# Cross-attention block on one core: place of the bias rows' picks, and order of the products in the projections of contexts

## What is computed

```
def _cross_attention(q_in, kv_in, wq, bq, wk, bk, wv, bv, wo, bo, bias_k, bias_v):
    qh = (q_in @ wq + bq).reshape(b, q_len, H, K)
    kh = (kv_in @ wk + bk).reshape(b, t, H, K)
    vh = (kv_in @ wv + bv).reshape(b, t, H, K)
    kh = concatenate([kh, bias_k], axis=1)      # one bias row behind the 1500 keys
    vh = concatenate([vh, bias_v], axis=1)
    logits = einsum('bqhk,bthk->bhqt', qh, kh) / scale
    weights = softmax(logits, axis=-1)
    ctx = einsum('bhqt,bthk->bqhk', weights, vh).reshape(b, q_len, H * K)
    return ctx @ wo + bo

x = x + _cross_attention(layer_norm(x), context, ...1)
x = x + _cross_attention(layer_norm(x), context, ...2)
x = x + gelu(layer_norm(x) @ w_fc1 + b_fc1) @ w_fc2 + b_fc2
```

## Time and profile before

| | us |
|---|---|
| three runs without profile, median (lowest to highest) | 1191.36 (1190.72 to 1191.61) |
| the profiled execution | 1191.98 |
| its span (first to last instruction) | 1190.2 |
| PE busy in the span | 1178.3 (99%) |
| PE weight loads busy | 1098.7 (92%) |
| DVE, POOL, ACT busy | 893.2, 870.5, 770.4 |
| share of PE in the chain that ended last | 95% |
| of it line 808 (scores) | 39% |
| of it line 773 (projections) | 6% |

### The profile page before, as it was taken

How to read it: one execution, slowest core, us unless ns; L and a number is a source line. 1 busy time by engine, 2 the same in 40 slices (tenths; PEclk the granted TensorE clock), 3 DMA queues, 4 the chain that set the end, 5 groups by cost and what they waited for, 6 DMA issues and landing times.

```text
span 1190.2 us, 26498 instructions
## 1 busy us (share of the span) xinstructions
PE 1178.3 (99%) x7664; PEld 1098.7 (92%) x7664; DVE 893.2 (75%) x1654; ACT 770.4 (65%) x1514; POOL 870.5 (73%) x741
## 2 busy tenths in 40 slices
PE   8999999999999999999999999999999999999999
PEld 7788999999999999998998999999999999999898
DVE  6888768686867687777786877777777777777854
ACT  6756666666666666676685666666666666667766
POOL 4659778787878788677552878787969696967772
PEclk9999999999999999999999999999999999999999
DMA  5311222222222222233330122222222222222331
GB/s 166 114 56 53 64 73 62 73 61 73 60 74 59 75 59 75 48 72 94 96 98 19 40 63 74 61 75 58 75 58 74 60 74 60 72 50 72 71 102 44
DMA packets 148299, 83.62 MB, mean 70 GB/s; under 512 B 121181, under 2 KB 122605, under 8 KB 148249
## 3 DMA queue, kind: packets, MB, share of 16 engines
q1 hardware_dynamic: 147560, 82.23, 26.8%
q10 hardware_dynamic: 688, 0.80, 0.2%
HBM read 68.56 MB, written 0.53 MB: 58 GB/s over the span
## 4 chain that ended last, share of the span: by engine, by line
PE 95%; DVE 2%; ACT 1%; issue 1%; DMA 1%; DVEq 0%; SPq 0%; ACTq 0%
PE psum L808 39%; PE psum L815 14%; PE psum L821 14%; PE psum L816 13%; PE psum L773 6%; PE psum L861 5%; PE psum L787 3%; PE psum L721 1%; DVE g_prod L1354 1%; PE psum L737 0%; DVE oth L1597 0%; PE psum L842 0%; ACT oth L1202 0%; PE psum L760 0%; DVE t_max L1463 0%
## 5 line engine op out<-in xcount | busy, mean ns | idle before, releaser
L628 POOL TENSOR_TENSOR pt<-slots,pt 125x512 fp32r<-125x512 f32 (+3 forms) x384 | 454.2, 1191 | 155.4 <-ACT slots L1125 149.4
L808 PE MATMUL psum<-qs,ctx 128*125 128x384 f32 (+1 forms) x2304 | 527.5, 367 | 0.4 <-ACT slots L1144 0.4
L808 PEld LDWEIGHTS psum<-qs,ctx 128*125 128x125 f32 x2304 | 397.2, 186 | 40.4 <-ACT slots L1144 1.0
L815 PE MATMUL psum<-ctx,pt 125*128 125x258 f32 (+1 forms) x1344 | 378.5, 283 | 0.7 <-ACT on L1132 0.6
L816 PE MATMUL psum<-ctx,pt 125*128 125x256 f32 (+1 forms) x1344 | 376.9, 282 | 0.0
L821 PE MATMUL psum<-ctx,pt 125*128 125x258 f32 (+1 forms) x1344 | 369.4, 282 | 0.0
L1122 ACT ACTIVATE pt<-slots 125x512 fp32r<-125x512 f32 (+3 forms) x384 | 221.5, 577 | 220.6 <-DVE slots L1447 216.5
L1463 DVE TENSOR_TENSOR t_max<-psum,t_max 125x512 f32<-125x512 f32 (+1 forms) x282 | 175.4, 622 | 152.6 <-PE psum L808 150.6
L815 PEld LDWEIGHTS psum<-ctx,pt 125*128 125x128 f32 (+1 forms) x1344 | 253.5, 189 | 12.9 <-ACT on L1132 2.5
L816 PEld LDWEIGHTS psum<-ctx,pt 125*128 125x128 f32 (+1 forms) x1344 | 254.2, 189 | 6.5
L821 PEld LDWEIGHTS psum<-ctx,pt 125*128 125x128 f32 (+1 forms) x1344 | 250.5, 190 | 0.3 <-POOL pt L628 0.2
(11 more groups left out here) (115 smaller groups left out, 1032.9 us busy)
## 6 DMA issues: line engine op xcount, KB each, us to landing
tr_stage<-ctx_tr SPq DMA_DIRECT2D x60, 375.0 KB, 3.2
nat_stage<-ctx_nat SPq DMA_DIRECT2D x60, 375.0 KB
w_raw<-weights SPq DMA_DIRECT2D x70, 256.0 KB, 2.7
qt<-turn SPq DMA_DIRECT2D x256, 32.0 KB, 2.0
qt<-turn SPq DMA_DIRECT2D x224, 24.0 KB, 1.9
dk_rest<-dk_rows SPq DMA_DIRECT2D x6, 256.0 KB, 3.9
w_raw<-weights ACTq DMA_DIRECT2D x2, 256.0 KB, 4.8
dk_first<-dk_rows SPq DMA_DIRECT2D x2, 256.0 KB, 3.4
```

Source lines behind the costliest of these rows:

```text
L628: nc.gpsimd.tensor_tensor(split_weights(h, LO, c), logits(h, c), as_f32(split_weights(h, HI, c)), ALU.subtract).then_inc(pt_lo, 1)
L808: last = mm(scores(h, k, first), ctx_tr_chunk(half, a, c), qs[h][:, m, half, 0:R], start=(half, a, m) == terms[0], stop=(half, a, m) == te ...
L815: mm(out_bank[:, 0:D + 2], hi, ctx_nat_hi(c), start=(c == 0), stop=False, skip_group_check=True)
```

## The change

Two things change, both on PE's list; no other engine's list is touched.

First, the matmuls of the picks, with the two waits ahead of them (`consts_in`, `pn_ready`), become a function that `first_contexts` calls behind the projection of head 0 and ahead of that of head 1. Second, in projections of contexts (those with `ready`) the order of the three products becomes HI x HI, LO x HI, HI x LO: weights' remainder second, context's remainder last. The waits go with their products: for `w_lo` before the second, for `oth_lo` before the third.

```diff
@@ project
                 pe.wait_ge(w_hi, INIT + job + 1)
-                for a, m in TERMS:
+                order = TERMS if ready is None else (TERMS[0], TERMS[2], TERMS[1])
+                for a, m in order:
                     if (a, m) == (LO, HI):
                         pe.wait_ge(w_lo, INIT + job + 1)
                     elif ready is not None:
...
                     for c in range(DC):
                         last = mm(out_bank, w[u][:, a, c * P:(c + 1) * P], moving(m, c),
-                                  start=(a, m, c) == (HI, HI, 0), stop=(not more and (a, m, c) == (LO, HI, DC - 1)))
+                                  start=(a, m, c) == (HI, HI, 0), stop=(not more and (a, m, c) == (*order[-1], DC - 1)))
@@ first_contexts
-            def first_contexts(n, job):
+            def first_contexts(n, job, picks):
 
                 for u in range(2):
                     pe.wait_ge(c_lo, INIT + n + u - 3)
                     project(C_BANK[u][:, 0:ROWS], u, job + u, lambda m, c, u=u: oth[u][:, m, c, :],
                             ((oth_hi, INIT + n + u + 1), (oth_lo, INIT + n + u + 1)), True).then_inc(oth_used, 1)
+                    if u == 0:
+                        picks()
@@ PE's list, behind the transposes
-                pe.wait_ge(consts_in, 16 * N_CONSTS)
-                pe.wait_ge(pn_ready, INIT + (l + 1) * GROUPS)
-                settle(pe)
-                for j in range(TQ):
-                    last = mm(PICK_BANK[0:EXTRA, j * NT:(j + 1) * NT], pick[:, j, :], pn_extra[:],
-                              start=(j == 0), stop=True, skip_group_check=True)
-                last.then_inc(pn_picked, 1)
+                def picks():
+
+                    pe.wait_ge(consts_in, 16 * N_CONSTS)
+                    pe.wait_ge(pn_ready, INIT + (l + 1) * GROUPS)
+                    settle(pe)
+                    for j in range(TQ):
+                        last = mm(PICK_BANK[0:EXTRA, j * NT:(j + 1) * NT], pick[:, j, :], pn_extra[:],
+                                  start=(j == 0), stop=True, skip_group_check=True)
+                    last.then_inc(pn_picked, 1)
+
                 heads, jobs = l * H, l * JOBS + H
-                first_contexts(heads, jobs)
+                first_contexts(heads, jobs, picks)
```

## The result

The changed kernel takes 1193.64 us (median of 19 runs, 1192.82 to 1194.66) against 1191.34 of the kernel before (19 runs, 1190.35 to 1192.58): ratio 1.0018, 95% interval 1.0012 to 1.0025. That is 2.3 us slower. The interval leaves out 1, so the loss is real, though it is just inside the 0.2% that the prediction calls no change. It is in the forecast range (1190.6 to 1193.8), and 0.9 more than the forecast of 1192.7. The profiled execution took 1194.57, with a span of 1192.8 (before: 1191.98 and 1190.2).

A forecast was written before the change was run, and what follows sets the result against it. PE, busy 99% of the span, bounds the kernel, so only its gaps can move. Per layer 0.83 - 0.41 + 0.26 = +0.68, for two layers +1.4 us, from median 1191.36 to 1192.7; range 1190.6 to 1193.8.

The forecast's parts named there:

- What bounds: PE is busy 99% of the span and makes 95% of the chain; the change can only move PE's gaps.
- Part 1: Picks behind head 0's projection, once per layer: DVE's remainder of head 2 is late, PE released 1.24 us later.
- the shift at head 2: Gap 1, passage from attention to output projections: the next product starts at 545.11 instead of 544.28, +0.83 us per layer.
- The queue on ACT: Head 2's context copy stands behind p80's copy, so DVE's remainder starts at 543.0 to 543.1 instead of 541.77.
- Rival 1: DVE's remainder of head 2 is not held up by POOL; total about 0, 1191.3 us; chance 0.18.
- Part 2: Context's remainder last in all 32 context projections: PE puts two more matmuls (0.41) before that wait, wants weights' remainder 0.41 earlier.
- Gain at head 2: Gap 1: PE waits for the context's remainder with two matmuls to come instead of four, saving 0.41 us.
- at head 4: Gap 2: PE waits for the same copy with two matmuls left and 0.06 to wait, -0.41 us per layer.
- Head 5: Its projection newly waits 0.16 for POOL's weight remainder, plus a restart of 0.10: +0.26 us per layer.
- The bounds of the sum: One layer between -0.16 and +0.83, both together -0.3 to +1.7 us; with the runs' scatter 1190.7 to 1193.5.
- Rival 2: The picks fill PE's waits, gaps 1 and 2 go, a new idle comes: -0.5 per layer, 1190.3 us; chance 0.10.
- Rival 3: Weights' remainder makes PE wait at each of 11 heads in two layers: 5.5 us slower, 1198.2; chance 0.05.

The follow-up runs named there:

- e5_act: Changed kernel with ACT's context copy of head 2 put ahead of its copy of p80: 1194.06 us, ratio 1.0019 against the kernel before.
- e4_w3: Changed kernel with POOL's weight remainder of head 3 held back until DVE has made head 2's context remainder: 1193.53 us, ratio 1.0012 against before.
- e2_order: Kernel before with only the order of the products changed, the picks left where they were: 1191.93 us, ratio 0.9999.
- e9: Kernel before with the new product order in all context projections, and POOL's masked values ahead of its weight remainders in the loop: 1191.10 us, ratio 0.9994.
- e8: Kernel before with context's remainder last for heads 0 to 4 only, and POOL's masked values ahead of its weight remainders in the loop: 1190.55 us, ratio 0.9988.
- e3_mask: Changed kernel with POOL's masked values of a head made before its weight remainder in the loop over heads 4 to 15: 1193.51 us, ratio 1.0013 against before.
- e1_picks: Kernel before with only the picks moved behind head 0's projection, the order of the products left: 1194.94 us, ratio 1.0025.
- e7_sel: Kernel before with the product with the context's remainder last for heads 0 to 4 only, picks unmoved: 1191.83 us, ratio 0.9998.
- e10_pool: e8 with POOL's weight remainders of heads 0 to 2 ahead of the masked values, head 3's behind DVE's remainder of head 2: 1189.28 us, ratio 0.9978.

## Why the prediction was right, and where it was not

**What bounds.** Right: in the medians only the passages show. Their sum, +2.2, is the measured +2.3. (The profiled executions have another difference, in layer 2's query stage; see the last section.)

**Part 1.** Right in its path and its sizes, with one reason told by half. With 0.21 added to the times of the changed kernel's profile: head 0's projection was forecast to start at 538.88 and started at 539.12, DVE's remainder of head 2 was to end at 544.55 and ended at 544.54, PE was to be released at 544.60 and was at 544.58, the shift at head 2 was to be 0.83 and is 0.81 and 0.77 (table). The 0.24 at the start is partly a DMA's: in layer 1 ACT waited for the last move of the contexts, and the gap from the last transpose was 1.40, against 1.26 in layer 2. It cost nothing further on, since head 2 hangs on POOL. The queue on ACT, which the prediction names as what makes DVE late, is not enough of a reason: with ACT early DVE still starts only 0.35 sooner (e5_act), because DVE's own list has the remainder of p80 ahead of head 2's. The prediction had that step's end at 542.76, 0.3 before its start of head 2's, and did not say that it holds DVE too. And the release does not come sooner at all, since the lock between POOL and DVE holds it, as e4_w3 shows. ACT's order and POOL's were not changed together in one run. Rival 1 (no lock) is out: the lock is worth 0.44 and 0.41 per layer in e4_w3, where the prediction had 0.58.

The Trainium skill, SBUF — State Buffer, section "Who interferes with whom", has the port pair as an exclusive lock which the later instruction waits for. The runs agree on who is held up: DVE in the changed kernel and in e5_act, where POOL began first, and not in e4_w3, where POOL is idle during head 2's remainder. They differ by about 0.14 us on how much: in the changed kernel DVE ends 0.96 after POOL (544.33 against 540.85 + 2.52 = 543.37) and in e5_act 0.94 (543.40 against 539.94 + 2.52 = 542.46), while it takes 1.09 alone. By the page's rule taken to the letter it would be 1.09. Not rounded, it is 0.95 (0.946 to 0.953) in all places of the thirteen profiles where such a remainder (128x896) takes 1.24 us or more. The profile's ends of POOL's instructions are rough, so whether the 0.14 lies in the engines or in the record stays open.

**Part 2.** Gain at head 2 (0.41 forecast, e2_order 0.43) and at head 4 (0.41, e2_order another 0.41): right. Head 5: the wait for the weight remainder was forecast at 0.26, and e9 against e8 has 0.27. The step that failed is the line "Head 5": it asked only when the weight remainder would be ready, and not what stands behind it on POOL. Those are head 5's masked values (L686). In the kernel before, they start 0.33 ahead of DVE's context remainder of head 6, take 0.40, and are ready long before PE's dvm product:

```profile
552.31 0.40 POOL L686 TENSOR_TENSOR dvm<-dv,mask 80x128 fp32r<-80x128 f32 x1
...
552.64 1.09 DVE L1597 TENSOR_TENSOR oth<-qt,oth 128x896 fp32r<-128x896 f32 x1 [0.18 <-ACT oth L1202]
...
553.46 0.37 PE L842 MATMUL psum<-p,dvm 80*128 80x448 f32 x1
```

In the changed kernel they start 0.09 behind DVE's remainder (552.93 against 552.84) and take 1.25. Counted from the last transpose, DVE's start has moved by 0.40 and POOL's by 0.83 (in e2_order by -0.85 and -0.41): DVE had the gain of head 4, POOL had not, and that exchanged the two. PE asks for the masked values at 554.24 - 0.31 = 553.93, and they are ready at 554.18. An estimate from these rows: with their 0.40 of before they would have been ready at 553.33, and PE would not have waited. No run tests that lengthening apart from their place behind the weight remainder: e3_mask and e8_selmask take both away from head 5. The missing term is 0.41 per layer, 0.8 in all, and it is nearly the whole 0.9 by which the forecast was short.

The bounds of the sum did not hold it: their upper end was +1.7, and the passages give +2.2. Nor do the prediction's times follow from its bounds: 1190.72 - 0.3 and 1191.61 + 1.7 are 1190.4 and 1193.3, where it has 1190.7 and 1193.5. The measured 1193.64 lies above both upper ends. Only the last widening, to 1193.8, for which no reason is given, held it. So the mechanism of the passage was right but for one term, but that the range held the time was luck.

**Rival 2** (both gaps vanish): out, by e1_picks. **Rival 3** (weights decide every head): out, by e2_order, where heads 6 and later show no wait. The spare of 0.49 in the loop was enough.

## What to carry to other kernels

If an instruction is moved on one engine, list for each engine that waits for it what is queued behind the wait; and if two engines hold each other up, as POOL and DVE do here, ask not only when each starts but which starts first, since a shift of some tenths can exchange them (here at heads 2 and 5). A step that is given an earlier due time must be checked with everything that the same consumer wants next from the same producer: here the weight remainder was looked at and the masked values behind it were not. And a gain ahead of a producer with its own pace is given back there: of e2_order's 0.84 per layer one queue took 0.7, and exchanging two steps of that queue (e8_selmask against e7_sel) was worth 0.67.

## What was not expected of the hardware

DVE's tiny copy of three columns (128x3) took 1.27 us when it began 0.02 behind the start of a POOL instruction, and 0.17 when only 0.13 of one was left (e10_pool, above). Over the thirteen profiles such copies (of three or four columns) took 0.16 to 0.17 in the 26 places where POOL was in no instruction when they began, and ended 0.02 to 0.03 after POOL's instruction wherever that had 0.25 us or more to go (212 places). So what such a copy loses is what is left of POOL's instruction, whatever its own size.

The query stage of layer 2, which the change does not touch, runs at one of two paces. Groups of six matmuls of 448 columns on PE, in the kernel before:

```profile
613.06 1.38 PE L787 MATMUL psum<-qh,w 128*128 128x448 f32 x6
614.28 1.38 PE L773 MATMUL psum<-ht,w 128*128 128x448 f32 x6
```

and in the changed kernel:

```profile
613.11 1.40 PE L774 MATMUL psum<-ht,w 128*128 128x448 f32 x6
614.35 1.40 PE L788 MATMUL psum<-qh,w 128*128 128x448 f32 x6
```

They follow each other in 1.22 and 1.24 us at the same granted clock (1.00). From the start of the first of the stage's 192 matmuls (L737) to that of the last (L787 or L788) this makes 38.95 against 39.70 us. (The two expectations below count the stage with 43.1 and 43.9 us, to a later end.) This is why the two profiled spans are 2.6 apart: 2.2 of the passages and 0.7 of this, less the 0.21 that the transposes were early and some rounding. To see whether it is a state of an execution, both kernels were profiled once more.

> The kernel before, unchanged, a second profile. In the profiles so far the query stage of layer 2 (no part of the change) takes 43.1 us in the kernel before and in e1_picks, 43.9 in the changed kernel and all others. If this is a state that an execution falls into, a second profile may show 43.9 here; if it hangs on the program, it shows 43.1 again.

> The changed kernel, unchanged, a second profile, for the same question: 43.9 again if the pace of layer 2's query stage hangs on the program, possibly 43.1 if it is a state of the execution. The passage should be 25.3 us in both layers again, with the same waits at heads 2, 4 and 5.

The second profiles show 38.95 and 39.70 again, and all thirteen profiles divide alike: 38.95 in the kernel before (twice) and e1_picks, which alone have the old order of the products in all projections, 39.70 in the ten others. So in profiled executions it hangs on the program. The cause is open, and whether it is there without a profile too is also open: the differences of the medians are those of the passages alone, within 0.5 us, without 0.7 on top. The passage itself repeated to 0.04 us: 24.25 and 24.21 for the kernel before, 25.37 and 25.34 for the changed one.
